# Routing 25 node tiles in five batches during the graph stage, and splitting expert 0 on GpSimd

## The chip, the cores and the metric

One core of a Trainium2 chip runs the kernel. Its engines are TensorE (PE in the profile), VectorE (DVE), ScalarE (ACT), GpSimd (POOL) and SyncE (SP, which here only issues DMAs). The metric is the device time of one execution in microseconds; the number given is the median of several.

## The reference, cut to what matters

3125 nodes with 256 features, 53125 edges sorted by destination. All is float32.

```python
x = x + gnn(layernorm(x), node_vec1_and_edges)     # attention over the edges of each node
h = layernorm(x)                                   # 3125 x 256
probs = softmax(h @ router_w.T)                    # 8 experts
topk_probs, topk_idx = top_k(probs, 2)             # ties: the lower expert
gates = one_hot_sum(topk_probs / (sum(topk_probs) + 1e-9), topk_idx)
y_e = (silu(h @ w1_e.T) * (h @ w3_e.T)) @ w2_e.T   # 682 hidden
out = x + sum_e gates[:, e] * y_e
```

## The kernel before, in words

Nodes stand in 25 tiles of 128 rows (`TILES`), 3125 of the 3200 rows being real; edges in 104 groups of 512 (`GROUPS`). The kernel has four parts.

**Set-up.** First layernorm, attention terms, a table `ztab` in HBM, edge scores.

**The stream over groups.** Each engine runs `run(engine, GROUPS, ..., stages)`: a list of stages, each with a lag; in turn T the engine executes, in the order of the list, each stage for group T minus its lag. All is written out and each engine runs its turns strictly in order; semaphores tie the engines together. GpSimd's only stage is `gather`: four indirect DMAs of 128 rows for each group (L780), into a ring of 12 groups, so that the gather of group t waits for `sums_psum` of group t-12. VectorE works out scores and one-hots (L1538 to L1607), TensorE the weighted sums (L1237) at lag 8. Every fourth turn a node tile j, whose edges are complete, passes through node stages at lags from 21 to 34 turns behind 4j: `node_parts` (L1165, L1168) on TensorE, `where_edge` (L1480) and `residual` on VectorE, layernorm (ScalarE stores x2 and the normed rows to HBM, `out` and `ttab`), router products (L1181), and last `logit_copy` (L1512) at turn 4j+34. The gathers end with group 103; what follows is the drain, in which the last groups and tiles 19 to 24 finish. VectorE then signals `stream_over` (L1626), on which SP loads experts 1 and 2 (2.1 MB each, L653, into `W`, where the stream worked before). Expert 0 was loaded at turn 44.

**Routing, all 25 tiles at once** (L1700 to L1819). VectorE waits for `logit_ready` 25 and for three ramps made on GpSimd. It works out softmax, first and second choice and gates on 200 columns (25 tiles by 8 experts); TensorE ranks the chosen rows inside tiles and counts them over tiles with two products (L1285, L1286); VectorE scans the counts, and gives each of the 2 x 25 choices a slot: 56 slots (`SLOTS`) of 128 rows, each slot of one expert. Each `link(...)` is an instruction followed by a wait for its own end. To turn "row to slot" into "slot to row", it makes one-hots of row-in-slot and slot number in bf16 (L1785 to L1792), and TensorE adds fifty products (L1290). VectorE decodes token numbers into `slot_rows`, waits for the gates to be in HBM (`gates_stored`), and signals `slots_ready`. SP stores the gates beside the normed rows (L733), behind its waits for the experts. ScalarE makes the high parts of experts 0 and 1 (`split_hi`), VectorE the low part of expert 0 (`split_lo`, L539) behind `slots_ready`, GpSimd that of expert 1 inside the expert loop.

**Experts.** For each of 56 slots: GpSimd gathers 128 rows from `ttab` (L831), TensorE transposes and multiplies with high and low parts (L1311, L1350), VectorE gates, GpSimd adds the rows to `out` (L824). Experts 3 to 7 are loaded by SP in eight chunks each, once `lo_split` says that the raw buffer is free.

The two ways `in_order` and `general` are two branches; sorted edges such as these take `in_order`.

Of the kernel before, what the change touches and what calls it, by code (L numbers as in the profile page):

```python
# [23 lines left out]

# [5 lines left out]
P = 128  # L30
N, C, EDGES, EF = 3125, 256, 53125, 64
E, H = 8, 682
# [53 lines left out]
S2 = 2 * TILES  # L86
RE = TILES * E
LATE = max(S2 * SLOTS + H + 2 * HPAD + NH * P + 2 * C, KC * NP)
# [3 lines left out]
assert GROUPS <= P and PAIRS % LOADS == 0 and AHEAD % BATCH == 0 and GROUPS % BATCH == 0  # L92
assert SLOTS % RING == 0 and GROUPS % 2 == 0 and SETTLED % BATCH == 0


def build(nc, x, src, src_batch, dst, dst_by_edge, dst_ends, mark_rows, wt, w_func, w_func_t, w_self_t, att_nodes, att_edge,
          router, experts, out):
    fp32, i32, bf16, fp32r = mybir.dt.float32, mybir.dt.int32, mybir.dt.bfloat16, mybir.dt.float32r
# [5 lines left out]
    with ExitStack() as ctx:  # L104
# [42 lines left out]
        tick = sb("tick", [P, 1])  # L147

        def carve(region, at, shape, dt=fp32):
# [4 lines left out]
            words = n if dt != bf16 else n // 2  # L154
# [33 lines left out]
        src_in, o = carve(ef, o, [LOADS, KG], i32)  # L188
        assert o <= 5 * WE
# [16 lines left out]
        io_i, o = carve(ef, o, [P], i32)  # L206
# [50 lines left out]
        ohr, o = carve(acc, 0, [S2, P], bf16)  # L257
        oht, o = carve(acc, o, [S2, SLOTS], bf16)
        iota_b, o = carve(acc, o, [P], bf16)
        slots_f, o = carve(acc, o, [S2])  # L260
        slots_i, o = carve(acc, o, [S2], i32)
        st_i, o = carve(acc, o, [S2], i32)
        sr_i, o = carve(acc, o, [S2], i32)
        st_f, o = carve(acc, o, [S2])
        sr_f, o = carve(acc, o, [S2])
        st_b, o = carve(acc, o, [S2], bf16)
        sr_b, o = carve(acc, o, [S2], bf16)
        tile_b, o = carve(acc, o, [S2], bf16)
        io_slot, o = carve(acc, o, [SLOTS], i32)
        slot_no, o = carve(acc, o, [SLOTS])  # L270
        slot_b, o = carve(acc, o, [SLOTS], bf16)
        tok, o = carve(acc, o, [SLOTS])
        unused, o = carve(acc, o, [SLOTS])
        row_f, o = carve(acc, o, [SLOTS])
# [4 lines left out]
        p_plus1, o = carve(acc, o, [1])  # L279
        dump_p, o = carve(acc, o, [1])  # L280
        io_p, o = carve(acc, o, [1], i32)
        exp_neg, o = carve(acc, o, [E])
        io_e, o = carve(acc, o, [E], i32)
        assert o <= TILES * ZR
        moving, behind = carve(late, 0, [S2, 2 * SLOTS], bf16)
        o = behind
        s_act, o = carve(late, o, [H])
# [3 lines left out]
        assert o <= LATE  # L291
        o = behind
# [239 lines left out]
        def split_lo(eng, v, e, piece):  # L532
            eng.wait_ge(hi_split, 2 * e + (1 + piece))
            if not isinstance(e, int):
                eng.wait_ge(lo_split[piece], e)
                held(eng)
            elif e > 0:
                eng.wait_ge(lo_split[piece], e)
# [1386 lines left out]
```

## Time and profile before

| | |
|---|---|
| median of 3 executions | 1058.42 us (1057.86 to 1058.95) |
| span of the profiled execution | 1057.7 us |
| busy: PE, DVE, ACT, POOL | 833.1, 619.6, 450.1, 575.1 us |
| chain that ended last: PE, DMA, issue, POOL, DVE | 54%, 11%, 11%, 10%, 9% |
| last logit copy | 614.79 us |
| slots known, first row gather, first expert product | 657.95, 658.86, 665.83 us |

Times in the rows are microseconds from the span's start, unless marked ns. "Busy" is time with an instruction at work. What stands in square brackets behind an instruction is the idle time of its engine just before it and what ended that.

### The profile page before, as it was taken

The numbers are of one execution on the slowest core, as the hardware profiler recorded it, in microseconds if no ns is written. First come the engines' busy times: TensorE is split into PE (matmuls) and PEld (weight loads), VectorE is DVE, ScalarE is ACT, GpSimd is POOL, SyncE is SP. The second block draws the span as 40 slices with busy tenths as digits, with TensorE's granted clock in tenths as the row PEclk, the third lists the DMA queues.
The fourth block names the chain that finished last, engine by engine and source line by source line (L and its number), as shares of the span: only waits on it lengthen the run. The fifth ranks groups of instructions, "written<-read, shape, count | busy, mean of one in ns | idle before, by whom it ended". The sixth has DMA issues, their size and how long they took to land.

```text
span 1057.7 us, 18646 instructions
## 1 busy us (share of the span) xinstructions
PE 833.1 (79%) x4388; PEld 695.9 (66%) x4389; DVE 619.6 (59%) x2073; ACT 450.1 (43%) x1063; POOL 575.1 (54%) x556
## 2 busy tenths in 40 slices
PE   7955879865865775775777921899999999999995
PEld 6812444644654664664565711899999999999995
DVE  6524555555665666666656668456566565656553
ACT  4323243464565456456456730234344343443331
POOL 1177777777777777777775000635353544434332
PEclk9986998987887888788788955899999999999998
DMA  7775666565554545555454250452534522222221
GB/s 241 209 250 187 189 199 183 143 180 173 149 141 133 148 133 141 141 142 143 133 158 116 68 190 1 124 114 48 115 67 89 116 44 46 35 41 40 40 41 20
DMA packets 81139, 128.83 MB, mean 122 GB/s; under 512 B 21356, under 2 KB 56689, under 8 KB 80577
## 3 DMA queue, kind: packets, MB, share of 16 engines
q0 software_dynamic: 30720, 69.90, 28.6%
q1 hardware_dynamic: 43145, 51.59, 15.7%
q10 hardware_dynamic: 7200, 6.56, 1.8%
q8 instruction: 22, 0.36, 0.1%
q14 instruction: 52, 0.43, 0.1%
HBM read 106.86 MB, written 17.86 MB: 118 GB/s over the span
## 4 chain that ended last, share of the span: by engine, by line
PE 54%; DMA 11%; issue 11%; POOL 10%; DVE 9%; DVEq 2%; POOLq 0%; ACT 0%; SPq 0%; ACTq 0%
PE bank L1311 17%; PE bank L1237 13%; POOL early L780 8%; DMA early<-ztab,early 8%; PE bank L1350 6%; PE bank L1201 3%; PE bank L1340 3%; PE bank L1357 2%; PE bank L1083 2%; PE bank L1168 2%; PE bank L1165 2%; PE bank L1099 1%; DMA out_rows<-late,slot_rows 1%; DVE acc L1607 1%; POOL out_rows L824 1%
## 5 line engine op out<-in xcount | busy, mean ns | idle before, releaser
L780 POOL DMA_INDIRECT early<-ztab,early x416 | 396.4, 953 | 173.2 <-issue 170.5
L1311 PE MATMUL bank<-split_w,operands 128*128 x1344 | 237.7, 326 | 2.8 <-DVE operands L1839 1.4
L1237 PE MATMUL bank<-early,W 128*128 128x258 f32 x832 | 232.4, 432 | 6.5 <-DVE W L1584 6.0
L1311 PEld LDWEIGHTS bank<-split_w,operands 128*128 128x128 f32 x1344 | 213.6, 190 | 9.4 <-issue 7.4
L1237 PEld LDWEIGHTS bank<-early,W 128*128 128x128 f32 x832 | 172.0, 216 | 55.0 <-issue 23.6
L831 POOL DMA_INDIRECT xg<-ttab,slot_rows x56 | 57.6, 1028 | 230.4 <-DVE late L1866 180.2
L982 ACT ACTIVATE W<-early 128x128 f32<-128x128 f32 x208 | 91.0, 484 | 128.1 <-PE bank L1237 124.7
L1201 PE MATMUL bank<-ident,early 128*16 128x128 f32 x104 | 24.2, 380 | 138.7 <-DVE early L1567 138.7
L1201 PEld LDWEIGHTS bank<-ident,early 128*16 128x16 f32 x104 | 10.3, 120 | 150.6 <-DVE early L1567 148.0
L824 POOL DMA_INDIRECT out_rows<-late,slot_rows x56 | 88.9, 1588 | 34.0 <-issue 15.6
L1052 ACT ACTIVATE late<-bank 128x384 f32<-128x384 f32 x56 | 27.5, 491 | 187.6 <-PE bank L1311 187.6
L1350 PE MATMUL bank<-split_w,operands 128*128 x336 | 96.7, 396 | 1.3 <-ACT operands L1059 1.3
L1538 DVE TENSOR_TENSOR early<-edge_sb,early 128x4 f32<-128x4 f32 x104 | 16.4, 157 | 104.1 <-DMA early<-ztab,early 95.6
L1825 DVE TENSOR_TENSOR late<-late,bank 128x384 f32<-128x384 f32 x56 | 31.0, 554 | 72.5 <-ACT late L1052 72.5
L971 ACT ACTIVATE early<-iota_row,W 128x128 f32<-128x128 f32 x208 | 70.6, 387 | 0.0
L1350 PEld LDWEIGHTS bank<-split_w,operands 128*128 128x128 f32 x336 | 60.3, 188 | 9.6 <-issue 2.0
L1863 DVE TENSOR_SCALAR late<-bank,xg 128x256 f32<-128x256 f32 x56 | 27.1, 484 | 66.6 <-DMA out_rows<-late,slot_rows 43.9
L1584 DVE TENSOR_SCALAR W<-iota_row,W,early 128x128 f32<-128x128 f32 x208 | 64.1, 355 | 0.7 <-ACT early L964 0.4
L1607 DVE SCALAR_TENSOR_TENSOR acc<-bank,W,acc 128x258 f32 x104 | 45.8, 481 | 31.3 <-issue 18.6
L1136 PE MATMUL bank<-W,xg 128*32 128x512 f32 (+2 forms) x104 | 53.0, 643 | 9.8 <-DMA W<-in_wt 5.7
L1848 DVE TENSOR_TENSOR operands<-bank,operands 128x512 fp32r<-128x512 f32 x112 | 49.7, 486 | 7.4 <-ACT operands L1058 2.9
L1532 DVE TENSOR_TENSOR_SCAN W<-W,bank 16x512 f32<-16x512 f32 x26 | 31.4, 1208 | 36.4 <-PE bank L1201 36.4
(232 smaller groups left out, 1320.8 us busy)
## 6 DMA issues: line engine op xcount, KB each, us to landing
W<-in_wt SPq DMA_DIRECT2D x26, 512.0 KB, 4.8
W<-in_experts SPq DMA_DIRECT2D x40, 266.5 KB, 2.8
early<-ztab,early POOLq DMA_INDIRECT x416, 2.8
W<-in_experts SPq DMA_DIRECT2D x3, 2132.0 KB, 11.7
early<-in_x SPq DMA_DIRECT2D x26, 128.0 KB, 2.2
early<-ztab SPq DMA_DIRECT2D x25, 128.0 KB
early<-late SPq DMA_DIRECT2D x25, 128.0 KB
out_rows<-early ACTq DMA_DIRECT2D x25, 128.0 KB, 1.9
```

The source lines that it names most:

```text
L780: nc.gpsimd.indirect_dma_start(out=zg[:, k * KG + c, :], out_offset=None, in_=ztab, in_offset=bass.IndirectOffsetOnAxis(ap=src_here[:, k / ...
L824: nc.gpsimd.indirect_dma_start(out=out, out_offset=bass.IndirectOffsetOnAxis(ap=slot_rows[:, 2 * t + 1:2 * t + 2], axis=0), in_=y_out[:, k ...
L831: nc.gpsimd.indirect_dma_start(out=xg[:, k, :], out_offset=None, in_=ttab, in_offset=bass.IndirectOffsetOnAxis(ap=slot_rows[:, 2 * t:2 * t ...
L971: last = nc.scalar.activation(dist[:, k % 2, c * P:(c + 1) * P], iota_row[:, :], ACT.Abs, bias=dst_at[:, cols(t * KG + c, 1)], scale=-1.0)
L982: last = nc.scalar.activation(prob_hot[:, k % 3, c * P:(c + 1) * P], dist[:, k % 2, c * P:(c + 1) * P], ACT.Relu, bias=prob[:, at:at + 1], ...
L1136: last = mm(ps[1][0:end - first, 0:G], att_pad[:, GROUPS - 2 - g:GROUPS - 2 - g + end - first], vec_in[:, n % W_RING, m * G:(m + 1) * G], ...
L1201: last = mm(ps[0][0:BC, i * P:(i + 1) * P], e_ring[:, at + lo:at + lo + BC], order[:, :], start=True, stop=True)
L1237: last = mm(ps[2 + k // 2 % 2][:, 0:ZR], prob_hot[:, k % 3, c * P:(c + 1) * P], zg[:, k * KG + c, :], start=(k % 2 == 0 and c == 0), stop= ...
L1311: last = mm(bank[:, 0:n], x[:, (k % 2 * KC + c) * P:(k % 2 * KC + c + 1) * P], split_w[:, bass.ds(at + (part + w + c * H), n)], start=(i = ...
L1350: return mm(ps[5][:, 0:2 * C].rearrange("p (b c) -> p b c", c=C), hidT_hi[:, i * P:(i + 1) * P], split_pairs[:, bass.ds(two, 2), W2_AT + i ...
L1584: last = v.tensor_scalar(prob_hot[:, k % 3, c * P:(c + 1) * P], iota_row[:, :], dst_at[:, cols(t * KG + c, 1)], prob[:, at:at + 1], ALU.is ...
L1607: v.scalar_tensor_tensor(acc[:, bass.ds(to, ZR)], ps[2 + k // 2 % 2][:, 0:ZR], of[:, cols(t - 1, 1)], acc[:, bass.ds(to, ZR)], ALU.mult, A ...
```

## The change: what it does

Routing runs in five batches of tiles: 0 to 6, 7 to 13, 14 to 19, 20 to 23, and 24. The first four are a new stage `route` at lag 34 in the stream of VectorE, TensorE and ScalarE: `early_route(t)` gives, from turn 34 + 4(hi-1) on, step i of the batch that ends before tile hi. The fifth, and all that needs all counts, is `route_rest(4)` behind the stream.

- Choices are made from the logits and not from the probabilities; first choice, second choice, ranks, gates and one-hots are steps of their own.
- A running `prefix` of counts is kept in place of the scan. A product with it and one with `before` give each choice one number, expert x 3200 + rank in the expert. Its low 8 bits are `row_of` (256 rows), the rest is `cell_f`: 100 cells (`HALF_CELLS`) of 256 rows, two slots' worth each.
- One-hots are fp16: `hot_row` of 256 columns, `hot_cell` of 100 columns times the token number. They go in chunks of 3 choices through a ring of two chunks, and TensorE adds them to bank 1 over the whole stream. At the end a last pair of products (`slots_of`) picks the cells for the 56 slots.
- `slots_ready` no longer waits for the gates' store; GpSimd waits for it (`gates_stored` 32). SP stores the gates in two parts, for tiles 0 to 23 and for tile 24, both behind its loads of experts 1 and 2.
- GpSimd splits expert 0 (both parts) behind the last sums of the stream; ScalarE splits the high part of expert 1 in turn 1 of the expert loop; VectorE's split of expert 0 is gone.
- SP waits for `raw_in` behind `finish_over`. The three late ramps of GpSimd are gone; two are made in set-up.

```diff
+ROUTES = ((0, 7), (7, 14), (14, 20), (20, TILES - 1), (TILES - 1, TILES))
+ROUTE_RING = 2
+CHUNK = 3
+CHUNKS_OF = [-(-2 * (hi - lo) // CHUNK) for lo, hi in ROUTES]
...
+        def split_first(pool):
+            pool.wait_ge(experts_in[0], 16)
+            for piece in range(2):
+                a, b = PIECES[piece]
+                nc.gpsimd.tensor_tensor(split(0, 0, piece), raw(0, piece), ones[:, 0:1].to_broadcast([P, b - a]), ALU.mult)\
+                    .then_inc(first_hi, 1)
+            for piece in range(2):
+                pool.wait_ge(first_hi, 1 + piece)
+                pool.sem_inc(hi_split, 1)
+                nc.gpsimd.tensor_tensor(split(0, 1, piece), raw(0, piece), split(0, 0, piece).bitcast(fp32), ALU.subtract)\
+                    .then_inc(lo_split[piece], 1)
...
+        def early_route(t):
+            for b, (lo, hi) in enumerate(ROUTES[:-1]):
+                i = t - BATCH * (hi - 1)
+                if 0 <= i < 5 + CHUNKS_OF[b]:
+                    return b, i
+            return None, None
...
@@ sync
-            for e in range(RAW):
-                sp.wait_ge(experts_in[e], 16)
-                sp.sem_inc(raw_in, 1)
-
+            early = ROUTES[-1][0]
+            gates_out = ttab[:, C:TR].rearrange("(t p) e -> p t e", p=P)
+            sp.wait_ge(gates_ready, len(ROUTES) - 1)
+            sp.dma_start(gates_out[:, 0:early, :], gates[:, 0:early, :]).then_inc(gates_stored, 16)
+            sp.wait_ge(gates_ready, len(ROUTES))
+            sp.dma_start(gates_out[:, early:TILES, :], gates[:, early:TILES, :]).then_inc(gates_stored, 16)
             sp.wait_ge(logit_ready, TILES)
...
             sp.sem_inc(finish_over, 1)
...
+            for e in range(RAW):
+                sp.wait_ge(experts_in[e], 16)
+                sp.sem_inc(raw_in, 1)
...
@@ gpsimd
                 run(pool, GROUPS, AHEAD, GROUPS // AHEAD, [(0, gather)])
+                pool.wait_ge(sums_psum, GROUPS)
+                split_first(pool)
...
             pool.wait_ge(finish_over, 1)
-            pool.wait_ge(gates_stored, 16)
+            pool.wait_ge(gates_stored, 32)
...
@@ tensor
+                for b, (lo, hi) in enumerate(ROUTES[:-1]):
+                    if in_stream and j == hi + 2:
+                        pe.wait_ge(choice_ready, 3 * b + 3)
...
+            def rank_of(b):
+                lo, hi = ROUTES[b]
+                n = hi - lo
+                pe.wait_ge(choice_ready, 3 * b + 1)
+                pe.wait_ge(or_idle, min(hi + 2, TILES))
+                mm(ps[6][:, C:C + n * E], before[:, :], both[:, 0:n * E], start=True, stop=False)
+                pe.wait_ge(choice_ready, 3 * b + 2)
+                last = mm(ps[6][:, C:C + n * E], ones[:, 0:P], prefix[:, 0:n * E], start=False, stop=True)
...
+                last.then_inc(rank_psum, 1)
+
+            def tokens_of(b, i):
+                pe.wait_ge(onehot_ready, chunk_no(b, i) + 1)
+                for q, j, at in chunk(b, i):
+                    last = mm(ps[1][0:HALF_CELLS, 0:2 * P], hot_cell[:, at, :], hot_row[:, at, :], start=(b == 0 and q == 0),
...
+                last.then_inc(token_psum, 1)
...
@@ vector
+            def second_choice(b):
...
+                dve.wait_ge(choice_ready, 3 * b + 1)
+                for i in range(n):
+                    added = v.tensor_tensor(prefix[:, (i + 1) * E:(i + 2) * E], prefix[:, i * E:(i + 1) * E],
+                                            both[:, i * E:(i + 1) * E], ALU.add)
+                    if i < n - 1:
+                        link(added)
+                added.then_inc(choice_ready, 1)
...
+            def one_hots(b, i):
+                if chunk_no(b, i) >= ROUTE_RING:
+                    dve.wait_ge(token_psum, chunk_no(b, i) - ROUTE_RING + 1)
+                for q, j, at in chunk(b, i):
+                    v.tensor_scalar(hot_row[:, at, :], iota_h, row_of[:, q:q + 1], None, ALU.is_equal)
+                    last = v.tensor_scalar(hot_cell[:, at, :], iota_h[:, 0:HALF_CELLS], cell_f[:, q:q + 1], token_id[:, j:j + 1],
+                                           ALU.is_equal, ALU.mult)
+                last.then_inc(onehot_ready, 1)
...
             def in_order():
+                def route(t, k, r):
+                    b, i = early_route(t)
+                    if i == 0:
+                        first_choice(b)
+                    elif i == 1:
+                        second_choice(b)
+                    elif i == 2:
+                        ranks_of(b)
+                    elif i == 3:
+                        gates_of(b)
+                    elif b is not None and i < 4 + CHUNKS_OF[b]:
+                        one_hots(b, i - 4)
...
                 v.memset(tick[:, :], 0.0).then_inc(stream_over, 1)
+                route_rest(len(ROUTES) - 1)
```

## Rows read from the trace of the kernel before

**Rows 1.** Stretches: from:to, length, busy us by engine, granted clock, DMA share, GB/s.
```profile
48.67:571.70 523.03, 368.35 (x1521) 262.89 (x1521) 299.73 (x1233) 250.78 (x616) 395.44 (x415) 0.85 0.57 161
571.70:614.96 43.26, 38.24 (x199) 31.79 (x198) 26.93 (x110) 30.75 (x77) 1.30 (x5) 0.97 0.25 75
614.96:665.83 50.87, 7.29 (x57) 6.03 (x57) 39.73 (x91) 10.49 (x8) 6.06 (x4) 0.50 0.30 102
665.83:1057.70 391.87, 378.39 (x2406) 355.93 (x2406) 222.64 (x509) 137.43 (x292) 169.60 (x117) 0.98 0.34 65
```

**Rows 2.** Chain of waits, 614 to 664 us: start, length, what.
```profile
614.96 2.67 issue
617.70 0.18 DVE acc L1713
...
636.90 6.82 DVE acc L1785
...
657.95 0.09 DVE split_w L539
...
658.86 4.82 DMA xg<-ttab,slot_rows
```

**Rows 3.** Timeline of VectorE, prices of single operations: start, length, line, operation.
```profile
601.45 0.41 DVE L1475 TENSOR_TENSOR early<-early 128x256 f32<-128x256 f32 x1
...
629.10 0.17 DVE L1748 TENSOR_TENSOR late<-late 128x8 f32<-128x8 f32 x1
629.31 0.18 DVE L1750 TENSOR_SCALAR late<-thr 128x25 f32<-128x25 f32 x1
...
633.97 0.19 DVE L1766 CAST acc<-acc 128x50 int32<-128x50 f32 x1
...
649.74 0.94 DVE L1792 TENSOR_SCALAR late<-acc 128x2800 bf16<-128x2800 bf16 x1
```

**Rows 4.** Issues and landings: SP and ScalarE from the timeline, then issues with us to landing.
```profile
615.00 1.14 SPq L653 DMA_DIRECT2D W<-in_experts  x2
629.33 7.59 ACT L530 ACTIVATE split_w<-W 128x2842 fp32r<-128x2842 f32 x4 [10.12 <-SPq L731]
...
ttab<-late SPq DMA_DIRECT2D x1, 100.0 KB, 3.8
xg<-in_atte SPq DMA_DIRECT2D x1, 0.2 KB, 9.4
```

**Rows 5.** Timeline of VectorE in the drain.
```profile
597.21 0.59 DVE L1584 TENSOR_SCALAR W<-iota_row,W,early 128x128 f32<-128x128 f32 x2
...
602.13 0.49 DVE L1480 SCALAR_TENSOR_TENSOR early<-bank,has_edge,early 128x256 f32<-128x256 f32 x1
...
605.65 0.49 DVE L1480 SCALAR_TENSOR_TENSOR early<-bank,has_edge,early 128x256 f32<-128x256 f32 x1 [0.65 <-PE bank L1168]
...
612.28 0.17 DVE L1512 COPY logits<-bank 128x8 f32<-128x8 f32 x1 [0.58 <-PE bank L1181]
614.79 0.17 DVE L1512 COPY logits<-bank 128x8 f32<-128x8 f32 x1 [2.34 <-PE bank L1181]
```

**Rows 6.** Timelines of VectorE, TensorE and GpSimd in one cycle of the stream.
```profile
358.85 0.17 DVE L1538 TENSOR_TENSOR early<-edge_sb,early 128x4 f32<-128x4 f32 x1 [2.12 <-DMA early<-ztab,early]
...
363.59 5.21 PE L1237 MATMUL bank<-early,W 128*128 128x258 f32 x16
...
372.00 0.95 POOL L780 DMA_INDIRECT early<-ztab,early  x1 [0.30 <-issue]
```

**Rows 7.** GpSimd's split by shape (busy us, mean ns), then VectorE beside and without it.
```profile
L539 POOL TENSOR_TENSOR split_w<-W,split_w 128x2842 fp32r<-128x2842 f32 x1 | 6.3, 6288 | 0.0
L539 POOL TENSOR_TENSOR split_w<-W,split_w 128x1422 fp32r<-128x1422 f32 x1 | 3.3, 3257 | 0.0
...
670.59 0.56 DVE L1825 TENSOR_TENSOR late<-late,bank 128x384 f32<-128x384 f32 x1 [5.18 <-ACT late L1052]
...
681.45 0.55 DVE L1825 TENSOR_TENSOR late<-late,bank 128x384 f32<-128x384 f32 x1 [1.55 <-ACT late L1052]
```

More of the change, by code:

```diff
@@ L153, in carve @@
                 n *= d
[L154 removed]
+            words = n if dt != fp16 else n // 2
             v = region[:, at:at + words]
@@ L1279, in general @@
                 run(pe, TILES, NODE_RING, TILES // NODE_RING, [(0, share_T), (1, node_parts), (5, hn2_T), (5, logits_of)])
+                route_rest(0)
             branch(pe, in_order, general)
-            pe.wait_ge(choice_ready, 1)
-            pe.wait_ge(pool_consts, 3)
-            chosen = both.rearrange("p t e -> p e t")
-            mm(ps[0][:, 0:RE], before[:, :], chosen, start=True, stop=True)
-            mm(ps[1][:, 0:RE], ones[:, 0:P], chosen, start=True, stop=True).then_inc(rank_psum, 1)
-            pe.wait_ge(onehot_ready, 1)
-            for q in range(S2):
-                last = mm(ps[2][:, 0:2 * SLOTS], ohr[:, q, :], moving[:, q, :], start=(q == 0),
-                          stop=(q == S2 - 1))
-            last.then_inc(token_psum, 1)
-            pe.wait_ge(slots_ready, 1)
+            pe.wait_ge(expert_ready, 1)
             def expert(t):
@@ new lines, in gates_of @@
+            def gates_of(b):
+                lo, hi, n, lg, over_e, view = tiles_of(b)
+                total, inv = per_tile[:, 2, 0:n], per_tile[:, 3, 0:n]
+                dve.wait_ge(exp_ready, b + 1)
+                link(v.tensor_reduce(total, view(ex), AX.X, ALU.add))
+                link(v.reciprocal(total, total))
+                link(v.tensor_tensor(view(shift_l), view(ex), over_e(total), ALU.mult))
+                link(v.tensor_tensor(view(rest), view(shift_l), view(both), ALU.mult))
+                link(v.tensor_reduce(inv, view(rest), AX.X, ALU.add))
+                link(v.tensor_scalar(inv, inv, 1e-9, None, ALU.add))
+                link(v.reciprocal(inv, inv))
+                v.tensor_tensor(gates[:, lo:hi, :], view(rest), over_e(inv), ALU.mult).then_inc(gates_ready, 1)
@@ L1732, in _ @@
-            link(v.tensor_tensor(both, top0, top1, ALU.add))
-            for top in (top0, top1):
-                v.tensor_tensor(top, top, over_e(valid[:, :]), ALU.mult)
-            link(v.tensor_tensor(both, both, over_e(valid[:, :]), ALU.mult))
-            v.memset(tick[:, :], 0.0).then_inc(choice_ready, 1)
-            link(v.tensor_tensor(t25[:, 5, :], t25[:, 2, :], t25[:, 3, :], ALU.add))
-            link(v.tensor_scalar(t25[:, 5, :], t25[:, 5, :], 1e-9, None, ALU.add))
-            link(v.reciprocal(t25[:, 5, :], t25[:, 5, :]))
@@ L1812, in _ @@
-            link(v.tensor_scalar(tok, tok, 0.0, None, ALU.max))
-            pair = slot_rows[:, :].rearrange("p (t c) -> p t c", c=2)
-            v.tensor_copy(pair[:, :, 0], tok)
-            link(v.tensor_copy(pair[:, :, 1], row_f))
-            link(v.memset(hid[:, :, H:HPAD], 0.0))
-            dve.wait_ge(gates_stored, 16)
-            v.memset(tick[:, :], 0.0).then_inc(slots_ready, 1)
-            for piece in range(2):
-                split_lo(dve, v, 0, piece)
+            dve.wait_ge(expert_ready, 1)
```

390 lines of the change are left out of this document (232 added, 158 removed).

## The prediction

> **What bounds the kernel now.** I read the stretches first, then the chain of waits, then the instruction lists of each stretch. There are four stretches after the set-up [rows 1]. From 48.67 to 571.70 us GpSimd issues 416 gathers at one pace and idles for nothing but its own issue. From 571.70 to 614.96 the last groups and the last node tiles drain. From 614.96 to 665.83 TensorE is busy for 7.29 us of 50.87: that is the routing. From 665.83 to the end, 391.87 us, TensorE is busy for 378 us with the experts, and nothing in the change gives it less to multiply. So the change can pay in the third stretch only, and can cost in the first two.
>
> In the third stretch the chain of waits is VectorE almost alone [rows 2]: 2.67 us of idle up to L1713, 19 us of small linked operations, the big one-hots from 636.90 (6.82 us for the first alone), the token products, and the last operations up to 657.95, when `slots_ready` is given. The first row gather is issued at 658.86 and takes 4.82 us, and the first expert product (L1311) starts at 665.83, 6.97 us after that issue [rows 1, 2]. Call S the moment of the `stream_over` tick behind the last logit copy (614.9 before): slots are ready at S+43, products start at S+50.9.
>
> **Tail with only tile 24 left.** A linked operation on 8 to 25 columns costs 0.21 us from start to start (629.10 to 629.31); one on 50 columns is 0.02 longer (0.19 for 0.17), so 0.23; an unlinked one I estimate at 0.1 [rows 3]. The trace has no fp16 `tensor_scalar` of 256 columns. From below: 2800 bf16 columns take 0.94 us, so 0.09 for 256; from above: 256 fp32 columns in `tensor_tensor` take 0.41. I take 0.15, nearer the first row, which is the same operation. Behind S: first choice 5 linked and one more, 1.1; second choice 9 linked, 2.0; gates 8, 1.7 (given at S+4.8); ranks 7 linked and some pairs, 1.7, the rank products being hidden by the gates; four one-hots 0.6; sizes to positions 8 linked and two picks, 1.9, which hide two token products and ScalarE's copy; two products and their wait 0.4; five operations 0.8. Slots are ready at S+10.2, 33 us earlier against S. `expert_ready` (2.6 us more) and the branch fit beside the gather. The 2.67 us at L1713 go, since this work stands ahead of the branch.
>
> **What ends the wait then.** GpSimd also waits for `gates_stored` 32. SP issues experts 1 and 2 behind `stream_over`, and both gate stores behind those on the same queue. The two loads, issued at 615.00, let GpSimd and ScalarE go on only near 629.1: S+14.1 (ScalarE, held by SP, starts at 629.33) [rows 4]. That a small transfer waits on this queue is shown at the start: 0.2 KB, issued behind the loads of x, landed 9.4 us after its issue. The gates' store with its rows of 32 B took 3.8 us from issue to landing; behind the loads I count 2.4 of it (the rest is latency that overlaps). So gates are stored at S+16.5, the gather starts 0.9 later (657.95 to 658.86), and products at S+16.5+0.9+6.97 = S+24.4. Expert 3's chunks now start at S+14 and run beside that gather; I add 1. **S+25.4, against S+50.9: 25.5 us.** The bounds: 6.3 less, if the stores were not held (S+10.2 decides), and 3 more if the loads and stores simply add.
> The Trainium skill (DMA: Bandwidth & Descriptors, Queues, rings and completion order) says that a ring is consumed in order on each engine but that completion isn't FIFO for the issuing engine. The late 0.2 KB agrees with the first half; by the second half the later store could still complete first, which is the rival without hold.
>
> **S itself moves.** Routing of tiles 14 to 19 and 20 to 23 falls into the drain. VectorE's order there [rows 5]: its turn 110 ends at 597.8.
> - Batch 2 (6 tiles, 48 columns, 0.23 a link): first choice 1.25, statistics 0.65, second choice 2.9 (its six prefix additions are linked, 1.2). The next sums start at 602.5. TensorE's node product of tile 22 stands behind the rank products and the mask product (`choice_ready` 9), so it starts at 603.65 and, at 1.75 us, ends at 605.4.
> - Ranks end at 604.7, the next node work 1.05, gates 1.8: 607.55. `where_edge` of tile 22 thus starts at 607.55 (602.13 before). Then 24 one-hots, 3.6 us, and 2.7 us of node work: tile 23's starts at 613.8 (605.65 before). That is +8.15, and the chain from there to tile 23's logit copy (6.6 us) is the old one: 612.28 becomes 620.4.
> - Batch 3 (4 tiles) stands ahead of the last logit copy: 1.2+2.45, 0.4 for the rank products, 1.3, gates 1.75: 627.5; the idle 2.34 us before 614.79 is covered by it. Its 16 one-hots, 2.4 us, stand behind the copy: S = 630.1, **+15.2**.
> Bounds: +8, if links cost 0.15 and one-hots 0.09; +26, if one-hots cost 0.41 (40 of them, 10 us more). TensorE, with longer gaps, may also fall to the lower level: 0.97 of full granted in the drain, 0.50, which is 1.2 GHz, in the routing [rows 1]. The node products of a tile (1.75 us) would then take twice that: up to 3.5 for two tiles, in the range only.
>
> **The stream.** Batches 0 and 1 (7 tiles) fall at turns 58 to 66 and 86 to 94. GpSimd's gather of group t waits for the sums of t-12. In such a cycle two groups' sums take 5.21 us from 363.59; the first ends near 365.9, and the gather that needs it, the 257th of the 416, is issued at 372.00: 6.1 us to spare, and more for the other three groups of the cycle [rows 6]. I cost batch 0 there, one cycle's times standing for all: first choice 1.3 and second choice 3.25 into idle of 1.5 and 2.12 (the second before 358.85), so turn 60 is 1.15 late; then VectorE waits for the rank products, which TensorE reaches only behind a group's sums (367.6): turn 61 is 5.3 late, with gates 1.9 and six one-hots (0.9) turn 64's scores 3.3 late. The sums of group 56 come at 389.4 for a gather at 392.0. 2.6 us are left, so 0 is my value. If one-hots cost 0.41 and a link 0.3, about 3 us are lost a batch.
>
> **Set-up and experts.** Some twelve small VectorE operations stand behind the start of the gathers; uncovered they would be 12 x 0.21 = 2.5 us late for the first group, whose ring has eleven more places to fill: 0. VectorE's split of expert 0 lay beside the first gather [rows 2]: removed, 0; its cover shrinks too, but that work is now done before. GpSimd splits it from 600 on: 2842 columns take 6.29 us, 1422 take 3.26 [rows 7], twice: 19.1 us, over at 619, before any use; 0, unless it stops VectorE (below). ScalarE's split of expert 1 (half of 7.59 us) [rows 4] lies beside the first expert products, 4.2 us: 0, at most 1.
>
> **Sum.** 1057.7 - 25.5 + 15.2 = 1047.4 us of span. The median of the runs, 1058.42, is 0.7 over the span: **1048.1**.
>
> **Rivals.**
> *GpSimd and VectorE stop each other (slower).* From 600 to 619 GpSimd runs four long instructions, just where VectorE does the work that moves S. Each one that held VectorE would hold it to its end, since linked work can't go round: 19.1 us, less some 2 of idle. Decides: one conflicting VectorE operation behind each start. 1048.1+17 = 1065. For it: VectorE's work there is all in SBUF with two inputs or one-input copies. Against: VectorE at 670.59, while GpSimd's split runs (665.95 to 675.43), takes 0.56 us, as it does at 681.45 without it (0.55) [rows 7]; but all VectorE operations there read PSUM, so the case isn't tried. Chance 0.25.
> The Trainium skill (SBUF — State Buffer, Who interferes with whom) says that a VectorE instruction with two SBUF inputs, or in a two-port mode, and a GpSimd instruction that reads SBUF lock each other out for a whole instruction. By that rule this rival happens; the PSUM rows agree with its exception and no more.
> *Gates not held.* For: the store may pass in its own time. Against: the late 0.2 KB. Gather at S+11, beside the expert loads, so 6.5 instead of 4.8 us, products at S+20: 1043. Chance 0.14.
> *The stream slips.* Both batches eat more than 6.1 us: 3 us each, 1054; at double the price of all links 1060. Chance 0.12.
> *It doesn't do what it says:* a drain that hides nothing and a tail paid twice, or the other branch taken; near 1058. Chance 0.04.
> The forecast has 0.45, its own range 1040 to 1055.
>
> **Numbers.** About 0.2% (2.1 us) is what can be told from no change. Faster: 0.43 of the forecast, 0.14, 0.09 of the stream's: 0.66. Slower: 0.25 of the first rival, 0.02 of the stream, 0.01: 0.28. Same: 0.06. Range: down to 1040 (forecast and most without hold), up to 1066 to take in the first rival.
>
> **What would show it.** In the trace after: `stream_over` near 630 (right), near 615 to 620 (the drain hid the work), near 648 (GpSimd held VectorE; single VectorE operations of 3 to 6 us between 600 and 620 would show it). Slots some 10 us behind it; GpSimd's first row gather some 17 behind it, with SP and not VectorE as what it waits for. Gathers without idle until near 572. TensorE from the first L1311 to the end in 392 us. The prediction is wrong if S moves by less than 8 or more than 26 us, or if the gather starts together with the slots.

## The result, and the profile after

The changed kernel takes 1071.53 us (median of 4 runs, 1069.12 to 1074.29), the kernel before 1058.14 beside it (1057.29 to 1058.95): 1.0122 times as long, interval 1.0103 to 1.0140. The forecast was 1048.1, faster; what happened is its first rival, GpSimd and VectorE stopping each other, priced at 1065. The profiled execution has a span of 1067.3 us (1057.7 before). All ratios below leave out a single execution of experiment 2 that took 2804 us, where the other three took 1069.2 to 1070.3.

The stretches come first, by core and time, in the columns of [rows 1]:

```profile
48.67:571.70 523.03, 372.38 (x1545) 268.51 (x1545) 322.70 (x1358) 250.27 (x617) 394.16 (x413) 0.85 0.56 160
571.70:600.00 28.30, 27.37 (x141) 23.53 (x140) 19.10 (x80) 22.28 (x55) 3.66 (x4) 0.99 0.26 71
600.00:620.00 20.00, 4.22 (x20) 3.20 (x20) 19.43 (x21) 5.75 (x11) 16.13 (x4) 0.66 0.11 34
620.00:640.00 20.00, 14.59 (x59) 11.79 (x60) 15.71 (x77) 5.19 (x13) 0.57 (x1) 0.66 0.08 27
640.00:660.00 20.00, 7.60 (x33) 5.46 (x32) 16.15 (x93) 3.16 (x7) 0.00 (x0) 0.60 0.32 112
680.00:1067.00 387.00, 373.80 (x2397) 352.48 (x2395) 222.60 (x509) 137.42 (x292) 167.92 (x116) 0.99 0.33 64
```

The third row is the odd one. From 600 to 620 VectorE is busy for 19.43 us with 21 instructions; in the next 20 us it does 77 in 15.71. A busy share of 97% is here a sign that it does nearly nothing. GpSimd's list (start, duration, line, operation, count) and then VectorE's, of those 20 us, show why:

```profile
603.87 7.44 POOL L558 TENSOR_TENSOR split_w<-W,ones 128x2842 fp32r<-128x2842 f32 x2 [27.60 <-PE bank L1347]
611.26 9.30 POOL L563 TENSOR_TENSOR split_w<-W,split_w 128x2842 fp32r<-128x2842 f32 x2
```

```profile
603.77 0.20 DVE L1661 TENSOR_REDUCE rt<-rt 128x6 f32<-128x48 f32 x1
604.01 4.84 DVE L1644 TENSOR_TENSOR rt<-rt 128x48 f32<-128x48 f32 x1
608.89 2.48 DVE L1645 TENSOR_TENSOR rt<-rt 128x48 f32<-128x48 f32 x1
611.40 0.20 DVE L1646 TENSOR_REDUCE rt<-rt 128x6 f32<-128x48 f32 x1
611.64 5.85 DVE L1647 TENSOR_TENSOR rt<-rt 128x48 f32<-128x48 f32 x1
617.53 3.07 DVE L1665 COPY rt<-rt 128x8 f32<-128x8 f32 x1
620.51 0.19 DVE L1666 TENSOR_TENSOR rt<-rt 128x48 f32<-128x48 f32 x1
```

Four operations that take 0.17 to 0.21 us elsewhere take 16.24 together, each up to the end of one of the four GpSimd instructions; a `TENSOR_REDUCE` between two of them passes in 0.20. The split isn't slowed: its two subtractions take 6.17 and 3.18 us here (6.29 and 3.26 in [rows 7]), and its two copies 4.92 and 2.56, so 16.7 and not the 19.1 that the prediction summed from subtractions alone. The split is over at 620.6, and at 620.51 VectorE is back at 0.19. TensorE stands behind it: its next product starts at 620.76 after 16.54 us of waiting, and the granted clock falls to 0.66.

Then the end of the routing. In these rows of SP (queue), VectorE and GpSimd, and of the chain of waits (start, duration, what), `stream_over` is at 653.96 (614.96 before, 630.1 forecast):

```profile
654.06 0.81 SPq L696 DMA_DIRECT2D W<-in_experts  x2
655.44 0.38 SPq L770 DMA_DIRECT2D ttab<-rt  x1
658.31 10.28 SPq L772 DMA_DIRECT2D ttab<-rt  x1
```

```profile
671.58 0.98 POOL L876 DMA_INDIRECT xg<-ttab,slot_rows  x1 [51.02 <-DMA ttab<-rt]
```

```profile
658.31 12.49 DMA ttab<-rt
670.83 0.75 issue
671.58 2.77 DMA xg<-ttab,slot_rows
...
676.60 4.20 PE bank L1411 x12
```

Against `stream_over` the routing behind it went nearly as forecast: the slots' table is ready at +10.1 (forecast 10.2, 43 before [rows 2]), the first gather waits for the gates' store and starts at +17.6 (17.4), the first expert product at +22.6 (25.4; the gather took 2.8 us, and not 4.8+1). From there to the end it is 390.7 us (391.87 before).

The stream slips too. GpSimd's gathers start 1.25 us apart with 0.30 us of idle between them, but for one in each batch's wake; those two, and the last gather of all:

```profile
392.53 0.94 POOL L826 DMA_INDIRECT early<-ztab,early  x1 [1.39 <-issue]
536.13 0.99 POOL L826 DMA_INDIRECT early<-ztab,early  x1 [2.56 <-issue]
575.33 0.94 POOL L826 DMA_INDIRECT early<-ztab,early  x1 [0.30 <-issue]
```

The two waits are 1.1 and 2.3 us over the usual idle, and the last gather is 3.3 us later than before (572.01). VectorE's own list shows the wait behind it, once in each batch:

```profile
368.14 0.27 DVE L1699 TENSOR_TENSOR rt<-rt,bank 128x112 f32<-128x112 f32 x1 [5.46 <-PE bank L1268]
511.64 0.27 DVE L1699 TENSOR_TENSOR rt<-rt,bank 128x112 f32<-128x112 f32 x1 [5.33 <-PE bank L1268]
```

### The profile page after: what moved, and what is told of

The parts are those of the page before. It is cut to its first block and busy times, and to the rows that moved or that the text cites. A ratio compares the mean times of both kernels' runs of the same rounds, so it can differ in the third digit from the quotient of the medians.

```text
span 1067.3 us, 18923 instructions
## 1 busy us (share of the span) xinstructions
PE 845.5 (79%) x4408; PEld 708.1 (66%) x4409; DVE 652.3 (61%) x2295; ACT 449.4 (42%) x1068; POOL 591.5 (55%) x558
## 5 line engine op out<-in xcount | busy, mean ns | idle before, releaser
L1347 PE MATMUL bank<-early,W 128*128 128x258 f32 x832 | 237.5, 439 | 11.3 <-DVE W L1846 8.4
L1347 PEld LDWEIGHTS bank<-early,W 128*128 128x128 f32 x832 | 174.6, 219 | 59.5 <-issue 27.5
L876 POOL DMA_INDIRECT xg<-ttab,slot_rows x56 | 55.4, 990 | 230.8 <-DVE late L2011 174.6
L869 POOL DMA_INDIRECT out_rows<-late,slot_rows x56 | 88.9, 1588 | 33.7 <-issue 16.1
L1869 DVE SCALAR_TENSOR_TENSOR acc<-bank,W,acc 128x258 f32 x104 | 45.8, 481 | 27.8 <-issue 16.9
L1020 ACT ACTIVATE early<-bank 128x32 f32<-128x32 f32 x26 | 5.1, 197 | 108.6 <-PE bank L1324 108.6
```

The source lines that it names most:

```text
L869: nc.gpsimd.indirect_dma_start(out=out, out_offset=bass.IndirectOffsetOnAxis(ap=slot_rows[:, 2 * t + 1:2 * t + 2], axis=0), in_=y_out[:, k ...
L876: nc.gpsimd.indirect_dma_start(out=xg[:, k, :], out_offset=None, in_=ttab, in_offset=bass.IndirectOffsetOnAxis(ap=slot_rows[:, 2 * t:2 * t ...
L1347: last = mm(ps[2 + k // 2 % 2][:, 0:ZR], prob_hot[:, k % 3, c * P:(c + 1) * P], zg[:, k * KG + c, :], start=(k % 2 == 0 and c == 0), stop= ...
L1869: v.scalar_tensor_tensor(acc[:, bass.ds(to, ZR)], ps[2 + k // 2 % 2][:, 0:ZR], of[:, cols(t - 1, 1)], acc[:, bass.ds(to, ZR)], ALU.mult, A ...
```

## The experiments

S is `stream_over`; the other columns are the first row gather and the first expert product behind it, and the span, all of the profiled execution; then the median of the runs. The ratio is to the kernel before, timed on the same chip beside it.

| kernel | S | gather | product | span | median | ratio (95%) |
|---|---|---|---|---|---|---|
| before | 614.96 | +43.9 | +50.9 | 1057.7 | 1058.14 | 1 |
| after | 653.96 | +17.6 | +22.6 | 1067.3 | 1071.53 | 1.0122 (1.0103 to 1.0140) |
| 1 split off GpSimd | 638.44 | +17.2 | +22.6 | 1052.0 | 1053.77 | 0.9933 (0.9916 to 0.9951) |
| 2 before, split on GpSimd | 626.63 | +44.0 | +49.0 | 1067.9 | 1070.01 | 1.0081 (1.0061 to 1.0101) |
| 3 GpSimd only writes | 648.10 | +16.9 | +23.2 | 1063.2 | 1065.11 | one run, none |
| 4 small pieces | 646.14 | +17.2 | +22.9 | 1061.6 | 1063.36 | 1.0022 (1.0010 to 1.0034) |
| 5 gates stored first | 637.61 | +14.5 | +22.6 | 1051.0 | 1054.34 | 0.9951 (0.9931 to 0.9970) |
| 6 ranks behind gates | 636.24 | +17.2 | +22.6 | 1051.6 | 1052.09 | 0.9929 (0.9904 to 0.9953) |
| 7 both (5 and 6) | 636.63 | +14.3 | +22.7 | 1050.9 | 1053.38 | 0.9942 (0.9925 to 0.9960) |
| 8 both, four batches | 628.66 | +16.1 | +23.0 | 1042.5 | 1045.01 | 0.9867 (0.9840 to 0.9893) |
| 9 both, three batches | 617.19 | +21.0 | +28.0 | 1037.2 | 1039.20 | 0.9814 (0.9797 to 0.9830) |
| 10 as 5, loads behind gather | 638.92 | +11.0 | +18.0 | 1054.4 | 1055.93 | 0.9969 (0.9960 to 0.9979) |
| 11 as 9, 17 tiles early | 617.27 | +19.8 | +26.8 | 1036.2 | 1039.27 | 0.9820 (0.9804 to 0.9837) |
| 12 as 1, three batches | 623.87 | +21.0 | +28.0 | 1043.0 | 1044.41 | 0.9861 (0.9827 to 0.9894) |

**1. The split taken off GpSimd.** The rest of the change stays; ScalarE and VectorE split expert 0 behind the routing.

```
-                split_first(pool)                       # GpSimd, both branches
+                act.wait_ge(experts_in[0], 16)          # ScalarE, in keep_tokens
+                split_hi(act, 0)
+                for piece in range(2):                  # VectorE, behind expert_ready
+                    split_lo(dve, v, 0, piece)
```

> The changed kernel with expert 0's split taken off GpSimd: ScalarE makes the high parts behind its last routing copy, VectorE the low parts behind expert_ready, both while the gates are awaited. Theory (GpSimd's long instructions hold VectorE from 604 to 620): no VectorE operation over 1.3 us in the drain, stream_over at about 654 - 17 = 637, first expert product at about 660, the whole 17 us faster than the changed kernel: 1050 to 1055, some 0.5% below the kernel before. Rival (the routing work in the drain is what costs, GpSimd's split only happens to lie there): L1644, L1645, L1647 and L1665 stay long or other work takes their place, and the time stays within 3 us of 1071.

Measured 1053.77 us (1052.65 to 1055.03). S comes 15.52 us earlier than in the changed kernel, and the four held operations had been 15.4 us over their usual 0.2 each (16.24 less 0.8). So the difference in S is the size of those four; in this trace no VectorE operation of the drain takes over 1.3 us. The cost of the split on GpSimd is shown.

**2. The split alone, on the kernel before.** Routing stays in one piece behind the stream. VectorE's split of expert 0's low parts is gone, and the late ramps are made in set-up.

```
+                pool.wait_ge(sums_psum, GROUPS)
+                split_first(pool)                       # GpSimd, ahead of finish_over
-            for e in range(2):
-                act.wait_ge(raw_in, e + 1)
-                split_hi(act, e)
+            act.wait_ge(raw_in, 2)
+            act.wait_ge(hi_split, 2)
+            split_hi(act, 1)
```

> The kernel before with only expert 0's split moved to GpSimd behind the last sums (and the three late ramps made in set-up, so that they don't stand behind it). Theory: VectorE's node work of 600 to 615 has two inputs in SBUF too and is held; the last logit copy moves from 615 to about 630, and the time rises by 12 to 16 us, to about 1072. Rival (only the many small linked routing operations suffer): the node work passes, the time stays within 2 us of 1058.

Measured 1070.01 (1060.25 before on that chip), a slowdown of some 9 us, somewhat under the 12 to 16 expected, without any of the new batches. The held operations in its VectorE list are the node stage's own:

```profile
600.65 3.78 DVE L1490 TENSOR_TENSOR early<-early 128x256 f32<-128x256 f32 x1
604.54 2.32 DVE L1522 SCALAR_TENSOR_TENSOR early<-early 128x1 f32<-128x1 f32 x1
607.29 5.96 DVE L1504 SCALAR_TENSOR_TENSOR early<-early 128x256 f32<-128x256 f32 x1
614.37 2.23 DVE L1490 TENSOR_TENSOR early<-early 128x256 f32<-128x256 f32 x1
```

Even `L1522`, one column wide, is held for 2.32 us: width doesn't matter, the two inputs in SBUF do. S moves by 11.7, the first product by 9.8, the span by 10.2. The product moves by less since the first gather takes 2.8 us here and 4.8 in the kernel before: more on that in 5.

**3. GpSimd only writes.** Ten memsets in place of the four instructions that read. The kernel leaves out the split of expert 0, so it computes something else and only its trace counts.

```
-                nc.gpsimd.tensor_tensor(split(0, 0, piece), raw(0, piece), ones[:, 0:1].to_broadcast(...), ALU.mult)
+                nc.gpsimd.memset(split(0, i % 2, 0).bitcast(fp32), 0.0).then_inc(first_hi, 1)
```

> The changed kernel with GpSimd's split replaced by ten memsets of the same regions, about as long in all; it leaves out the split of expert 0, whose weights become zero. Theory A (an instruction of GpSimd that only writes holds VectorE only where VectorE copies in a two-port mode): VectorE's tensor_tensor operations keep 0.2 us, at most one-input copies or tensor_scalar wait; stream_over near 637 to 642. Theory B (any long GpSimd instruction holds VectorE): operations of 2 us and more as in the changed kernel, stream_over near 650.

GpSimd runs them from 603.14 to 625.5, 22.3 us against 16.7. VectorE's list beside it:

```profile
604.03 0.21 DVE L1646 TENSOR_TENSOR rt<-rt 128x48 f32<-128x48 f32 x1
604.28 1.36 DVE L1664 COPY rt<-rt 128x8 f32<-128x8 f32 x1
608.90 1.57 DVE L1702 CAST rt<-rt 128x12 int32<-128x12 f32 x1
610.51 2.40 DVE L1703 TENSOR_SCALAR rt<-rt 128x12 int32<-128x12 int32 x1
612.96 2.40 DVE L1705 CAST rt<-rt 128x12 f32<-128x12 int32 x1
615.79 0.41 DVE L1588 TENSOR_TENSOR early<-early 128x256 f32<-128x256 f32 x1
...
620.23 2.57 DVE L1715 TENSOR_SCALAR xg<-early,rt 128x256 f16<-128x256 f16 x1
```

Two-input operations now take their usual 0.21 and 0.41 us; copies, casts and a `tensor_scalar` are held to the end of a memset. So there are two conflicts: an instruction that reads, with two-input operations; one that writes, with one-input copies and their like. (That `COPY` was held in the changed kernel too fits the second, since the split also writes. The `tensor_tensor` started at 604.36 behind the held `COPY` ends with it, after 1.28 us.) The Trainium skill (SBUF — State Buffer, Who interferes with whom) states both, and these rows agree. The size was missed: with reading gone the drain was to be nearly whole, but S is 9.7 us later than in 1, because the routing is full of copies, casts and one-hots.

**4. The same split in pieces of a sixteenth.**

```
-                nc.gpsimd.tensor_tensor(split(0, 0, piece), raw(0, piece), ...)
+                for a, b in parts[piece]:               # 16 of them
+                    nc.gpsimd.tensor_tensor(split(0, 0, piece)[:, a:b], raw(0, piece)[:, a:b], ...)
```

> The changed kernel with each of GpSimd's four split instructions cut into sixteen of 178 or 89 columns. Theory (VectorE waits for the end of one whole GpSimd instruction, then has its turn): no VectorE operation waits more than about 0.6 us, VectorE gets some 60 turns instead of 4, and stream_over comes at 640 to 646 instead of 654; time about 1058 to 1063. Rival (what is lost is GpSimd's total work, however it is cut): stream_over stays at 652 to 656 and the time at 1071.

```profile
603.59 11.96 POOL L560 TENSOR_TENSOR split_w<-W,ones 128x177 fp32r<-128x177 f32 x32 [27.02 <-PE bank L1355]
615.51 14.22 POOL L567 TENSOR_TENSOR split_w<-W,split_w 128x177 fp32r<-128x177 f32 x32
```

GpSimd now takes 26.2 us and not 16.7, and nothing on VectorE is held for long (linked operations of 0.2 us take up to 0.42, one-hots of 0.3 up to 0.64). S is 7.8 us earlier than in the changed kernel and 7.7 later than in 1. Held VectorE work costs by the GpSimd instruction's length; cutting it halves the loss and doesn't remove it.

**5. The gates stored first.** On 1. SP stores the gates of tiles 0 to 23 ahead of its wait for the stream, ScalarE's queue takes those of tile 24.

```
+                sp.wait_ge(gates_ready, len(ROUTES) - 1)
+                sp.dma_start(gates_out[:, 0:early, :], ...)      # now ahead of:
                 sp.wait_ge(stream_over, 1)
...
+                act.wait_ge(gates_ready, len(ROUTES))            # ScalarE, in keep_tokens
+                act.dma_start(gates_out[:, early:TILES, :], ...)
```

> The change with expert 0's split off GpSimd (e1), and the gates' stores moved: those of tiles 0 to 23 leave SP's queue before SP waits for stream_over, the last tile's leave ScalarE's queue ahead of its wait for the stream. Theory A (what ends GpSimd's wait for the first gather of the slots is the gates' table, whose last store stands on SP's queue behind expert 1's two loads): the first gather moves from 17.2 us behind stream_over to 11 or 12 us behind it, the gather itself takes 3 to 6.5 us because it now runs beside the loads, and the kernel takes 1048 to 1050 us against 1053.8. Theory B (the slots' table or the loads' traffic sets that time whatever queue the gates leave by): first product of the experts within 1 us of e1's 22.6 us behind stream_over, kernel within 1 us of e1.

The first product is at S+22.6, as in 1. From the chain of waits:

```profile
641.98 9.38 DMA ttab<-rt
...
652.14 5.78 DMA xg<-ttab,slot_rows
```

The store left by another queue and still took 9.4 us, against 12.1 in 1: the place in SP's queue is worth some 3 us of it (10 shows what the rest is). The gather started 2.7 us earlier, but took 5.8 us, 2.7 more than the 3.1 of 1. So the numbers are theory B's, but its reason is only part of it. The loads weren't beside that gather: from 651.4 to 656 the DMA engines move 0.06 MB. VectorE was. Its split of expert 0's low parts and GpSimd's instruction for the gather, from this run's lists:

```profile
650.23 4.59 DVE L551 TENSOR_TENSOR split_w<-W,split_w 128x2842 fp32r<-128x2842 f32 x2
652.14 3.50 POOL L877 DMA_INDIRECT xg<-ttab,slot_rows  x1 [76.48 <-DMA ttab<-rt]
```

The kernel before has the same pair, and 2, which has no such split on VectorE, only the gather:

```profile
657.95 3.11 DVE L539 TENSOR_TENSOR split_w<-W,split_w 128x2842 fp32r<-128x2842 f32 x1
658.86 3.03 POOL L831 DMA_INDIRECT xg<-ttab,slot_rows  x1 [48.34 <-DVE tick L1819]
670.65 0.99 POOL L846 DMA_INDIRECT xg<-ttab,slot_rows  x1 [54.34 <-DVE tick L1834]
```

Beside the split the gather's instruction takes 3.0 to 3.8 us (before, 5, 7) and ends 0.8 us behind an instruction of the split; with none beside it 0.94 to 1.00 (after, 1 to 4, 6), and the first gather's rows land 2.8 to 4.1 us after its start instead of 4.8 to 6.2. The hold works both ways: here VectorE's long two-input instruction holds GpSimd. Experiment 5 with VectorE's split elsewhere wasn't run.

**10. The loads behind the first gather**, on 5, tests that.

```
-                for e in range(len(EXPERTS_AFTER), RAW):
-                    expert_load(e)
...
             sp.sem_inc(finish_over, 1)
+            sp.wait_ge(row_gathered[0], 16)
+            for e in range(1, RAW):
+                expert_load(e)
```

> The gates stored ahead of the wait for the stream (the first of the two gate experiments) with the loads of experts 1 and 2 issued only when the first gather of the slots has landed. There the last tile's gates left by ScalarE's queue and yet landed 9.4 us after their issue, and the gather took 5.8 us. Theory A (the two 2.1 MB loads fill the DMA engines, and a small store behind them waits on whichever queue): the store lands in 2 to 4 us, the first gather is issued when the slots are ready, about 10 us behind stream_over (11 with issue), takes 2 to 3 us, and the first product comes 15 to 17 us behind stream_over and not 22.6: kernel 1045 to 1047 us, the loads still landing ahead of expert 1. Theory B (a store or gather of this kind takes this long of itself after the stream): within 1 us of 1054.3.

```profile
649.90 2.81 DMA xg<-ttab,slot_rows
652.72 8.42 DMA W<-in_experts
661.20 3.85 ACT split_w L542 x2
...
668.20 3.91 PE bank L1420 x12
```

Measured 1055.93 us, against 1045 to 1047 expected. The gates' last store now lands 1.4 us after its issue: the loads in flight were what held it, by either queue. The first gather starts at S+11.0, released by the slots' table, and takes 2.8 us, its instruction over before VectorE's split starts (the third gather's stands beside it and takes 4.56 us). The first product comes at S+18.0 rather than at 15 to 17, since VectorE's 4.59 us for expert 0's low parts (651.55 to 656.1) stand ahead of its operands. Then the gain is lost: ScalarE waits 7.19 us for expert 1's weights to split them, and expert 0's next activation is queued behind that split, so TensorE goes on only at 668.20, after a wait of 4.92 us. The hold by the loads paid for something: the weights being there.

**6. The ranks behind the gates**, on 1, so that VectorE works while TensorE makes the rank products.

```
                     elif i == 2:
-                        ranks_of(b)
+                        gates_of(b)
                     elif i == 3:
-                        gates_of(b)
+                        ranks_of(b)
```

> e1 with VectorE's second and third routing step exchanged: the gates' arithmetic comes ahead of the step that reads TensorE's rank product. Theory A (the gathers of the stream end 3.3 us later than before because VectorE stands up to 5.5 us before that product and the stream's own work is behind it): the last gather starts near 572 us and not 575.3, the wait is gone, stream_over is ticked near 635, the kernel takes 1050 to 1051 us. Theory B (the slip comes from the one-hots' and the routing's added work as such, on VectorE or TensorE, and not from the wait): last gather at 574 to 576, kernel within 1 us of e1's 1053.8.

**7. Both.** 5 and 6 together.

> e1 with both edits (gates stored first, ranks behind gates). If the two costs are apart from each other, one ahead of stream_over and one behind it, their gains add up: 1044 to 1047 us. If they share something (the batch that ends last sets both), the gain is that of the larger alone, 1048 to 1050.

In 6 the last gather starts at 571.10 (576.18 in 1) and the wait is gone from VectorE's list: the cause of the slip is shown. But S comes only 2.2 us earlier, and in time 6, 7 and 1 can't be told apart (0.9929, 0.9942 and 0.9933, intervals of 0.2% each way). The sum that 7 was to show isn't there: neither its 1044 to 1047 nor the 1048 to 1050. Of 5's part, VectorE's split takes the earlier start back (gather +14.3, its instruction 3.77 us). Where the gathers' gain went is in the drain: `where_edge` of tile 21 is 4.9 us earlier than in 1 (595.50 against 600.43), that of tile 22 only 2.0 (610.62 against 612.61), and VectorE idles for 3.29 us before it, 0.23 in 1. It seems that with the ranks last nothing on VectorE is left to cover TensorE's node product, which waits for them; no run tests that by itself.

**8. Four batches**, on 7: the batch between the last two node stages goes back behind them.

```
-ROUTES = ((0, 7), (7, 14), (14, 20), (20, TILES - 1), (TILES - 1, TILES))
+ROUTES = ((0, 7), (7, 14), (14, 20), (20, TILES))
```

> e7 with four batches, 0-6, 7-13, 14-19 and 20-24: nothing is routed between the last node stages, all five last tiles behind the last of them. Theory A (moving a batch in between the node stages delays stream_over by about its whole VectorE work, as the sum of the prediction had it: 8 of 15.2 us): stream_over 8 to 10 us earlier, the routing behind it about 5 us longer, kernel 0 to 5 us below e7. Theory B (the work between the node stages fills idle time of VectorE, so it costs little): stream_over less than 4 us earlier, the tail 5 longer, kernel 1 to 4 us above e7.

S comes 8.0 us earlier; the tail of five tiles ends in slots at S+16, and the first product is at S+23.0, against S+22.7 for one tile: those 6 us lie under the gates' store, held by the loads, and VectorE's split. Measured 1045.01, 8.4 below 7 and more than the 0 to 5 expected. Of what is left of the shift of S (628.66 against 614.96, 13.7 us) most is batch 2; 9 shows 2.2 that stay without it. TensorE's list there:

```profile
606.45 2.04 PE L1243 MATMUL bank<-wself_sb,early 128*128 128x256 f32 x4 [4.10 <-DVE rt L1708]
615.52 1.92 PE L1243 MATMUL bank<-wself_sb,early 128*128 128x256 f32 x4
```

The node product of tile 22 waits 4.10 us until VectorE has read the ranks out of the bank that it writes. The four products of that line take 2.04 us there and, for tile 23, 1.92; in the kernel before they took 1.03 (L1165 at 600.20). The granted clock of 600 to 615 is 0.73 where it was 0.91 before. Part of this is 6's order: in 1, with the ranks ahead of the gates, the same product (608.64) waits 1.40 us and its four take 1.10, though those of tile 23 (617.49) take 1.91 there too.

**9. Three batches**, on 7: nothing in the drain, nine tiles behind the last logit copy. One working buffer (`cand`) lies elsewhere to make room.

```
+ROUTES = ((0, 8), (8, 16), (16, TILES))
```

> Gates stored first, ranks behind gates, expert 0's split off GpSimd, and three batches, 0-7, 8-15 and 16-24: nothing is routed between the last node stages, nine tiles behind the last logit copy. Theory A (a batch between the node stages costs more than its own VectorE time, since TensorE waits 4.1 us there for the ranks to be read out of its bank and then runs the stages' products at half the clock, 2.04 us for four and not 1.03; with four batches stream_over is 628.7, 13.7 us later than before): with none there stream_over is at 614 to 617 as before, the slots are ready 20 us behind it (5 tiles take 16.0, four more about 1 us each), the first product of the experts comes at 641 to 644 against 651.7, kernel 1035 to 1038 us. Theory B (stream_over is late because of the work moved into the stream, not because of the batch in the drain): stream_over at 621 or later, kernel 1042 us or more.

Measured 1039.20 us (1038.83 to 1039.66), a little over the 1035 to 1038 expected: no version is faster. The granted clock of 571.7 to 614 is 1.00. S is 2.2 us later than before, against 13.7 with batch 2 in the drain: 11.5 apart. Behind it (GpSimd's list):

```profile
638.22 0.95 POOL L877 DMA_INDIRECT xg<-ttab,slot_rows  x1 [65.46 <-DVE slot_rows L1756]
```

The slots' table, not the gates, now releases the gather, at S+21.0. The product is at 645.22, S+28.0, 1.2 us beyond what was expected, and the time as much: again VectorE's part of the split (639.88 to 644.5) stands ahead of the operands. Putting it elsewhere wasn't tried here.

**11. 17 tiles early.** `ROUTES = ((0, 8), (8, 17), (17, TILES))`.

> As the last, with batches 0-7, 8-16 and 17-24: one tile fewer behind the last logit copy, its batch two groups of four later. Theory A (what matters is that the batch ends ahead of the last node stages): one-hots of that batch would reach to the stage of tile 21, so stream_over 1 to 3 us later than with 16 tiles, the tail 1 us shorter: kernel 0 to 2 us slower. Theory B (only the number of tiles behind the end matters): 1 us faster.

1039.27 us, no difference that can be measured from 9: S is the same, the tail 1.2 us shorter.

**12. Three batches without 5 and 6.** The batches of 9 on 1.

> The change with the split off GpSimd and three batches, 0-7, 8-15 and 16-24, and neither of the two other edits: all gates leave SP's queue behind the loads, the ranks stand ahead of the gates. Theory A (those two edits carry next to nothing here: with nine tiles behind the last logit copy the slots are ready 20 to 21 us behind stream_over, later than the gates' last store, which landed 16 to 17 us behind it): first gather released by the slots' table, kernel 1039 to 1042 us, at most 3 us above the version with both edits. Theory B (the gates' store, issued behind the loads, still ends that wait, or VectorE's wait for the ranks in the stream is repeated in the longer batch): first gather 2 us or more later behind stream_over, or stream_over at 620 or later, kernel 1043 us or more.

Half of each theory: the gather is released by the slots' table at S+21.0, so the place of the gates' store is worth nothing; but S is 6.7 us later than in 9, and the kernel 5 us slower. In VectorE's list

```profile
390.04 0.29 DVE L1699 TENSOR_TENSOR early<-rt,bank 128x128 f32<-128x128 f32 x1 [5.23 <-PE bank L1268]
553.47 0.29 DVE L1699 TENSOR_TENSOR early<-rt,bank 128x128 f32<-128x128 f32 x1 [5.67 <-PE bank L1268]
```

the wait of 6's theory stands again. The exchange that gained nothing measurable on 1, where the drain swallowed it, is worth some 5 us where nothing else stands in the drain. (12 and 9 differ in both edits; that the 5 us are the exchange's rests on these waits and on the gates' store ending no wait in either.)

## Why the prediction was wrong

- **The split on GpSimd: the step that failed.** The prediction put it at "0, unless it stops VectorE", and gave that case 0.25. It cost 15.5 us of S (1) and about 10 by itself on the old kernel (2). The rival's mechanism, place and price (+17) were right, and so were the sign rows: single VectorE operations of 2.5 to 5.9 us between 600 and 620 (3 to 6 forecast), and `stream_over` later even than the 648 named. The trace offered as evidence against it [rows 7] was, as the text said, of operations that read PSUM; it tested nothing about two inputs in SBUF, and the sentence of the Trainium skill (SBUF — State Buffer, Who interferes with whom) that the prediction set beside it named just this case. The chance should have followed it.
- **S without that.** Forecast +15.2, measured +23.5 (1). Three terms were too small. The stream: put at 0, measured 3.3 us at the last gather (4.2 in 1), by the very wait for the rank products that the prediction found (turn 61 "5.3 late"; waits of 5.46 and 5.33 measured) and took for covered. Batch 2: put at 8.15, measured 11.5 to 13.7 with the stream mended (8 against 9 and against before), in 6's order of steps; in the forecast's own order it wasn't measured by itself. The slower clock behind TensorE's wait stood only in the range. One-hots: 0.15 each, 0.30 a pair; a pair took 0.41 from start to start, so the 40 one-hots (20 pairs) are some 2 us more, part of batch 2's size and of the next. Batch 3: put at 7.05, measured 8.0 (7 against 8), right within one us. The terms overlap: mending the stream brought its last gather forward by 5.1 us and S by 2.2 (6 against 1).
- **The tail.** Slots +10.2 (10.1), gates stored and gather issued +17.4 (17.6), products +25.4 (22.6): right but for the gather, which took 2.8 us and not 5.8. The 4.8 us of the kernel before had 2 us of hold by VectorE's split in them, and taking that split away was put at 0; the 1 us for expert 3's loads was nothing. That the wait would be for the gates was right; their place in SP's queue was some 3 us of it and the loads in flight the rest (5, 10). That the store would need 2.4 of its 3.8 us behind the loads was a guess that no row backs, and came out right (stored at +16.8, 16.5 forecast). SP was named as what the gather would be seen to wait for, and it is its store.
- **The experts.** 390.7 against 391.87: nothing gained or lost.
- **The sum** 1047.4, +15.5 (split), +8.3 (rest of S), -2.8 (tail), -1.2 (experts), is 1067.2, the span after being 1067.3.

## What to carry to other kernels

An engine with idle time isn't free to give work to: before a long GpSimd instruction goes beside VectorE, look at what VectorE does in that window (two inputs in SBUF, copies, casts), and price it at the GpSimd instruction's full length. Look the other way too: a long two-input instruction of VectorE holds a gather that GpSimd is to issue. Work moved out of a serial tail pays where it lands in idle time that nobody waits behind; a batch of six tiles cost 11.5 to 13.7 us between the last node stages, where TensorE waits for it and its next products take twice as long, and two of eight inside the stream cost 2.2, once VectorE no longer waited there for TensorE. Behind a tail that something else ends (here two loads of 2.1 MB), five tiles cost no more than one, so shorten it only as far as that.

## What the runs showed of the hardware

- Which VectorE operations a GpSimd instruction holds depends on whether that one reads: reading held two-input operations, down to one column (2.32 us); memsets held copies, casts and `tensor_scalar` (1.4 to 2.6 us) and let two-input ones pass at 0.21 us. `TENSOR_REDUCE` passed at 0.20 us in both. GpSimd's own split was not slowed.
- The other way round, VectorE's two-input split of 2842 and 1422 columns held GpSimd's indirect gather: its instruction took 3.03 to 4.57 us beside it (before, 5, 7 to 12) and 0.94 to 1.00 with none beside it (after, 1 to 4, 6).
- The same 8,528 columns took GpSimd 16.7 us in four instructions and 26.2 in 64.
- A store of some 4 KB issued behind two loads of 2.1 MB landed 12.1 to 12.5 us after its issue on their queue, 9.4 on another engine's, and 1.4 when the loads were issued behind it (10).
- The fp16 `tensor_scalar` of 256 columns takes 0.28 us, 0.19 from start to start; the rows of before had bounded it by 0.09 and 0.41.
